# A state space scan: GpSimd's product and its sum are put behind marks that VectorE sets

## The reference, cut to what matters

```python
zxbcdt = jnp.einsum('bld,ed->ble', x_norm, in_proj_w)      # z, x_ssm, Bm, Cm, dt
dA = jnp.minimum(jnp.exp(dt * A), 0.99)
def step(h, inp):
    x_t, B_t, C_t, dA_t = inp
    h = jnp.clip(dA_t[:, :, None, None] * h + einsum('bhp,bn->bhpn', x_t, B_t), -10., 10.)
    return (h, einsum('bn,bhpn->bhp', C_t, h))
_, y = lax.scan(step, 0, (x, B, C, dA))                    # 2048 steps, 4 heads of 64, state of 64
y = y + x_multi * Dparam[None, None, :, None]              # the product D times x and its sum
y = layernorm(y * silu(z)) ; y = layernorm(clip(einsum(y, out_proj_w)))
```

## Time and profile before

| | |
|---|---|
| median of 3 runs | 1819.15 us (1818.82 to 1821.85) |
| the profiled execution: own time | 1810.79 us |
| its span | 1808.7 us |
| mean granted TensorE clock | 0.975 of full speed |
| TensorE busy | 1701.5 us (94%) |
| VectorE busy | 1607.2 us (89%) |
| ScalarE busy | 1476.5 us (82%) |
| GpSimd busy | 653.6 us (36%) |
| sums L1862, 16 of them | 25.4 us |

### The profile page before, as it was taken

One profiled execution on the slowest core, in us unless ns is written; L12 is line 12 of the kernel. 1 busy time (PEld: TensorE's weight loads), 2 busy tenths in 40 slices (PEclk: granted clock), 3 DMA queues, 4 the chain that ended last, 5 costly groups with the idle time before them and its releaser, 6 DMA issues.

```text
span 1808.7 us, 40081 instructions
## 1 busy us (share of the span) xinstructions
PE 1701.5 (94%) x15396; PEld 658.2 (36%) x15396; DVE 1607.2 (89%) x2294; ACT 1476.5 (82%) x2806; POOL 653.6 (36%) x932
## 2 busy tenths in 40 slices
PE   6899999999999999999999999999999799899784
PEld 4432222222222222278622222222222345466553
DVE  7899999999999999945499999999997587699778
ACT  5679999999999999943399999999999567767455
POOL 1433310222444444100045565556501133133437
PEclk9999999999999999999999999999999999899798
DMA  4523222111221122278512211221102343422121
GB/s 127 175 71 85 87 65 69 57 58 35 71 61 56 57 67 66 73 209 228 143 51 64 55 45 52 59 63 47 41 10 58 90 134 97 138 65 63 42 63 47
DMA packets 152765, 142.15 MB, mean 79 GB/s; under 512 B 40394, under 2 KB 131533, under 8 KB 152418
## 3 DMA queue, kind: packets, MB, share of 16 engines
q1 hardware_dynamic: 144226, 122.37, 23.5%
q0 software_dynamic: 8352, 17.29, 3.3%
HBM read 76.60 MB, written 60.03 MB: 76 GB/s over the span
## 4 chain that ended last, share of the span: by engine, by line
PE 77%; DVE 10%; ACT 9%; issue 2%; POOL 1%; DMA 0%; POOLq 0%; DVEq 0%; ACTq 0%
PE PS L2027 30%; PE PS L2126 18%; PE PS L2011 11%; ACT probs L1347 6%; PE PS L2076 4%; PE PS L2061 2%; PE PS L2170 1%; PE PS L2176 1%; PE PS L2249 1%; DVE mxp L907 1%; DVE hst L1119 1%; PE PS L2053 1%; DVE VP L1094 1%; DVE MXV L1125 1%; PE PS L2331 1%
## 5 line engine op out<-in xcount | busy, mean ns | idle before, releaser
L907 DVE TENSOR_REDUCE mxp<-PS 128x1 f32<-128x1024 f32 x1024 | 1170.1, 1212 | 16.3 <-PE PS L2011 10.4
L1347 ACT ACTIVATE probs<-PS 128x512 f32<-128x512 f32 x2048 | 1096.3, 597 | 61.2 <-PE PS L2126 14.7
L2027 PE MATMUL PS<-probs,VH 128*32 128x256 f32 x8192 | 642.5, 391 | 1.8 <-ACT probs L1347 1.0
L2126 PE MATMUL PS<-stacks 51*128 51x512 bf16 x2048 | 438.5, 387 | 20.2 <-ACT probs L1347 16.4
L2011 PE MATMUL PS<-stacks 48*128 48x512 bf16 x2048 | 416.2, 380 | 2.2 <-DVE mxp L907 1.2
L2027 PEld LDWEIGHTS PS<-probs,VH 128*32 128x32 f32 x8192 | 173.1, 108 | 412.1 <-issue 229.7
L2126 PEld LDWEIGHTS PS<-stacks 51*128 51x128 bf16 x2048 | 115.0, 93 | 460.0 <-ACT probs L1347 421.5
L1713 POOL DMA_INDIRECT S<-oe_d,ROWI x128 | 130.0, 1015 | 130.0 <-PE PS L2027 124.1
L1683 POOL DMA_INDIRECT xe_d<-S,ROWI x128 | 125.4, 980 | 135.7 <-PE PS L2027 113.9
L1661 POOL CAST spl<-nmx 128x8 bf16<-128x8 f32 x64 | 12.7, 199 | 304.8 <-DVE nmx L863 226.6
L2011 PEld LDWEIGHTS PS<-stacks 48*128 48x128 bf16 x2048 | 106.0, 95 | 10.5 <-DVE mxp L907 5.8
(11 more groups left out here) (363 smaller groups left out, 1852.1 us busy)
## 6 DMA issues: line engine op xcount, KB each, us to landing
stacks<-qkl_d SPq DMA_DIRECT2D x128, 96.0 KB
xe_d<-zt SPq DMA_DIRECT2D x16, 640.0 KB
XNT<-xe_d SPq DMA_DIRECT2D x32, 320.0 KB, 3.8
oe_d<-XNT SPq DMA_DIRECT2D x32, 320.0 KB, 3.2
stacks<-qkl_d SPq DMA_DIRECT2D x128, 64.0 KB
o_d<-SG SPq DMA_DIRECT2D x256, 32.0 KB
ews<-in_ew_dram SPq DMA_DIRECT2D x33, 192.0 KB, 2.4
stacks<-qkl_d SPq DMA_DIRECT2D x128, 32.0 KB
```

What stands on the lines that cost most here:

```text
L907: v.tensor_reduce(mxp[:, n // 2, n % 2:n % 2 + 1], MXB[n % 2].rearrange("p a c -> p (a c)"), X_AX, ALU.max).then_inc(mx_done, 1)
L1347: act.activation(probs[:, at:at + 512], PS[:, bank_of(u, e), :], ACT.Exp, scale=float(1.0 / np.sqrt(np.float32(DK)))).then_inc(exp_done, 1)
L2027: mm = pe.matmul(OB[32 * jg:32 * jg + 32, c:c + 256], VH[w][:, kt, :], probs[:, at:at + 256], start=(kt < 2 and half == 0), stop=(kt >= TC ...
L2126: pe.matmul(PS[:, bank_of(u, e), :], KS[w][o:o + KROWS + 3, kt * P:(kt + 1) * P], QS[w][o:o + KROWS + 3, q0:q0 + 512], start=True, stop=Tr ...
```

## The change

GpSimd's two operations per chunk are put elsewhere in time, and their order on its queue is changed. VectorE marks the end of the second L1106 (operand B made) on `bd_set`, and the end of L1119 (state scaled) on `hst_set`. Both are semaphores of the attention stage used again, which stand at 64 by then (`HALVES`). The product for chunk c waits for `bd_set` of chunk c. The sum for chunk c waits for `hst_set` of chunk c besides `y_out`. The product for chunk c+1 is issued ahead of the sum for c. VectorE's wait behind L1119 is now on `hst_set` and not on its own chain. The arithmetic is the same.

```diff
+        bd_set, hst_set, HALVES = nmx_ready, spl_ready, 2 * UNITS
...
                 for b in range(B):
                     bb = BS[c % 4][:, b, :].unsqueeze(1).broadcast_to([P, NH1, DS])
-                    v.tensor_tensor(BD[w][:, b, :, :], DE[:, b * NH1:(b + 1) * NH1, P - 1:P].broadcast_to([P, NH1, DS]), bb, ALU.mult)
+                    ins = v.tensor_tensor(BD[w][:, b, :, :], DE[:, b * NH1:(b + 1) * NH1, P - 1:P].broadcast_to([P, NH1, DS]), bb, ALU.mult)
+                ins.then_inc(bd_set, 1)
...
             def chunk_state(c):
-                link(v.tensor_tensor(hst2[:, :, :], HS[:, :, :], E2[c % 2][:, :, P - 1:P].broadcast_to([P, NH1, HP]), ALU.mult))
+                v.tensor_tensor(hst2[:, :, :], HS[:, :, :], E2[c % 2][:, :, P - 1:P].broadcast_to([P, NH1, HP]), ALU.mult).then_inc(hst_set, 1)
+                v.wait_ge(hst_set, HALVES + c + 1)
                 v.wait_ge(y_out, c + 1)
...
+            by_batch = lambda t: t.rearrange("p (b n) -> p b n", b=B)
+
+            def scaled_x(c):
+                pool.wait_ge(tile_ld[c % 4], TILE_BASE + 96 * (c // 4 + 1))
+                after(pool, xd_done, XD_BASE + c - 1 if c >= 2 else 0)
+                pool.wait_ge(bd_set, HALVES + c + 1)
+                pool.tensor_tensor(by_batch(XD[c % 2]), by_batch(XS[c % 4]), sc_aff[:, 0, :].unsqueeze(1).broadcast_to([P, B, DI]), ALU.mult).then_inc(xd_made, 1)
+
+            scaled_x(0)
             for c in range(TCH):
-                xd, w = XD[c % 2], c % 4
-                pool.wait_ge(tile_ld[w], TILE_BASE + 96 * (c // 4 + 1))
-                after(pool, xd_done, XD_BASE + c - 1 if c >= 2 else 0)
-                pool.tensor_tensor(xd.rearrange("p (b n) -> p b n", b=B), XS[w].rearrange("p (b n) -> p b n", b=B),
-                                   sc_aff[:, 0, :].unsqueeze(1).broadcast_to([P, B, DI]), ALU.mult).then_inc(xd_made, 1)
+                if c + 1 < TCH:
+                    scaled_x(c + 1)
                 pool.wait_ge(xd_made, XM_BASE + c + 1)
                 pool.wait_ge(y_out, c + 1)
+                pool.wait_ge(hst_set, HALVES + c + 1)
                 yc = YS.rearrange("p (b c) n -> p b c n", b=B)[:, :, c, :]
-                pool.tensor_tensor(yc, yc, xd.rearrange("p (b n) -> p b n", b=B), ALU.add).then_inc(xd_done, 1)
+                pool.tensor_tensor(yc, yc, by_batch(XD[c % 2]), ALU.add).then_inc(xd_done, 1)
```

## The result

The changed kernel took 1807.99 us, median of 5 runs (1803.81 to 1809.53), against 1819.15 before (5 runs, 1816.38 to 1823.96): a ratio of 0.9929, 95% interval 0.9908 to 0.995. Two repetitions gave 0.9945 (0.9927 to 0.9962) and 0.9941 (0.9918 to 0.9964). So the change is 10 to 13 us faster by the three ratios, and the 6.4 us forecast were too few; 1807.99 lies just under the range (1808.5 to 1816.5). The kernel before spreads over 13 us from run to run (1812.2 to 1825.59 in one set of 20 later runs), the changed one over 7 (1803.81 to 1810.99 in 9), which the three runs shown before did not reveal.

What follows compares the result with a forecast made beforehand. TensorE, at 8.09 us a chunk, was taken to bound the scan, just above VectorE. Removed waits of 4.89 us plus 1.53 us in the last chunk gave 6.4 us: 1819.15 to 1812.7 us, range 1808.5 to 1816.5.

Steps and rivals of the forecast that it cites:

- The bound: Scan of block 1: TensorE's own 8.09 us a chunk sets the period, just above VectorE's 8.0 us.
- Rival (a): VectorE bounds the scan and all its lost time returns, 16.1 to about 19 us: 1800 to 1803 us; chance 0.05.
- L1119's hold and the slack: Scan chunks: L1119 falls from 1.48 to 0.41 us; VectorE idles 1.16 us, the state has 1.25 us to spare.
- 4.89 + 1.53: Gain in us: six TensorE waits inside the scan vanish (4.89), and the last chunk's wait shrinks (1.53).
- Rival (c): The hold only moves, from L1119 to L1121 or L1125: about 1817 us; chance 0.10 with other small-gain ways.
- The indirect DMAs: L1094, held beside GpSimd's two indirect DMAs, ends 2.09 us late, under 2.41, so the 1.42 us wait vanishes.
- The clock: Last chunk: TensorE's clock still falls in the 2.03 us gap; waits of 1.42 us and less do not lower it.
- the term 0: Clock gain taken as 0 for the last chunk, with up to 3.1 us kept for the range.
- Rival (d): Slower: the clock falls inside the scan, 5.0 us per chunk, 1822.7 us with two such chunks; chance 0.04.
- Ahead of the scan: Chunk 0, before TensorE reaches L2329: L1116 may be held by 0.3 us, counted as nothing.
- The range: Whole kernel: 1808.5 us, clock holding in the last chunk with 1 us of spread, up to 1816.5 us.

Runs made afterwards that it cites:

- product-only kernel: Changed kernel with only the product waiting, for bd_set and ahead of the sum, while the sum starts with y_out as before: 1808.73 us, ratio 0.9946.
- the sum alone: Changed kernel with only the sum waiting for hst_set and the product back behind the previous chunk's sum, without bd_set: 1804.85 us, ratio 0.9928.
- the filled kernel before: Kernel before the change with three unused 128 x 512 matmuls on TensorE in front of the last chunk's: 1812.6 us, ratio 0.9976.
- the one with the delay in series: Changed kernel with one unused VectorE instruction of 1.2 us per chunk between L1121 and the new state: median 1818.86 us.
- the one with a single gap: Changed kernel with 2 us of unused VectorE work before the new state of chunk 2 only: median 1811.74 us, ratio 0.9965.

## Why the prediction was right or wrong

**The bound, right.** TensorE's quiet chunk is 8.09 us in every profile in which VectorE is the faster one, and 19 us of added VectorE work left it there. Rival (a), 16 us and more, did not come.

**L1119's hold and the slack, right.** The scaled state (now L1121) takes 0.42 us, VectorE idles 1.03 us (1.16 forecast), the state matmul starts 2.82 us after the last L1113 (2.81 forecast). All six waits within the scan went, and the last fell from 3.56 to 2.04 (2.03 forecast). Together 8.45 - 2.04 = 6.41 us against 4.89 + 1.53. Rival (c) fell: L1124 and L1128 run beside the sum at 0.42 and 0.68 us each, as L1121 and L1125 did.

**The indirect DMAs: right result, wrong reason.** I had read that the DMAs hold L1094. In the product-only kernel L1095 began 0.47 us after the start of the second DMA (0.46 before), with no product behind it, and took 1.23 us. With the sum alone, where a product does stand behind the DMAs, VectorE was held again, this time in operand B (2.59 us for two instructions of 0.75 together):

```profile
1629.71 1.03 POOL L1875 DMA_INDIRECT ews<-in_ew_dram,rows  x1 [0.30 <-issue]
1630.18 1.23 DVE L1095 TENSOR_TENSOR VP<-cst,ldc 128x1024 f32<-128x1024 f32 x1
```

```profile
1628.50 2.59 DVE L1107 TENSOR_TENSOR YM<-VP,probs 128x256 f32<-128x256 f32 x2
1629.51 1.29 POOL L1860 TENSOR_TENSOR VH<-SG,sc_aff 128x512 f32<-128x512 f32 x1
```

So the hold came from the product queued directly behind them. What the Trainium skill infers in SBUF — State Buffer, Who interferes with whom, that a tensor_tensor leaves descriptor generation alone, agrees with the first of these rows (1.03 us beside L1095). It doesn't agree with four other profiles, in which the second DMA took 2.08 or 2.09 us beside L1103 (last section).

**The clock, wrong.** The step that failed is the sentence that the gaps of 1.42 us and less did not bring the clock down, and with it the term 0. It rested on one execution. Of three profiles of the kernel before, two have the clock down inside the scan, for 6.8 and 10.2 us; so have the filled kernel before (6.8), the one with the delay in series (10.2) and the one with a single gap (10.2). Of eight profiles of kernels without a wait over 1 us there, six have none and two 3.4 us, in the router's chunk both times. Three profiles of each kernel give 129.95 and 120.75 us, 9.2 less: 6.15 us of waits (8.19 to 2.04), 0.4 us that stand behind them in the first profile too, with the clock up (some 0.07 at each of six), and 2.6 us of clock, which I had at nothing. The last chunk gave 0.4 us more (7.42 to 6.99). Rival (d) had this mechanism with the sign reversed: it stood in the kernel before, and the change took it away.

**Ahead of the scan, put at nothing without a reason.** For chunk 0 I had weighed only a hold of L1116. But the first product held L1070: 0.51, 0.40 and 1.03 us in the three profiles of the kernel before, 0.16 in the three of the changed one. TensorE's wait before the second sums fell from 1.55 us on average to 1.14, and from chunk 0's turning matmul to the first state matmul it took 7.9 us before and 6.6 after. That is 1.3 us, most of it clock: it was down in this stretch in all three of the one and in one of the three of the other. The sum is 9.2 + 0.4 + 1.3 = 10.9 us, against 10 to 13 by the ratios, whose intervals reach from 6.5 to 17 us.

**The range.** It ended 0.5 us above the measured median. Its lower end took the clock's gain for the last chunk only, and 1 us of spread, less than the runs have.

What stays open is how often the clock falls in the unprofiled runs, and so what it is worth on average; the profiles are too few for more than some 3 us. That a wait brings it down is shown by no single profile: five of six with a wait over 1 us against two of eight without is what speaks for it, and all five fell in the router's chunk, whose small matmuls may have a part in it (two kernels fell there without such a wait). Only the fall behind the indirect DMAs, after 1.47 us of waiting, came in another chunk. A wait put back in a chunk without the router's rows was not tried. The 1.3 us ahead of the scan rest on three profiles of each kernel as well.

## What to carry to other kernels

Two engines that are within a few per cent of each other hide what the second one loses, until a disturbance uses up the slack: price such a hold by the waits it lets through, not by its length. And price a wait of TensorE by its length plus what its clock may lose behind it, from more than one execution. Put GpSimd's two-input operations where VectorE waits or reads PSUM, the one first whose collision lies on the way to the state (here the sum, which made the whole gain), and order both queues so that neither holds the other back.

## What the runs showed of the hardware

A single wait of 1.42 us was followed by 10.2 us at 1.2 GHz and cost 6.2 us; in the first profile of the kernel before waits of 1.42, 1.16 and 0.88 us cost 0.07 us beyond themselves. Whether the clock falls differs between executions of the same program.

A small copy of 8 elements with one SBUF input was held 1.0 us by GpSimd's product, where instructions with one input in PSUM and one in SBUF were never held (0.42 us each for L1121 and L1124). The Trainium skill says that a copy can run in a 2-port mode and then contends with GpSimd (SBUF — State Buffer, Who interferes with whom). The copy's 0.16 against 1.13 us agrees; which mode it ran in no row shows. A subtraction of 16 elements on one partition (L1070) was held up to 0.87 us by a product of 1.27.

Of GpSimd's indirect DMAs the second started 0.03 to 0.04 us after L1103 in eight profiles. In four of them it took 2.08 or 2.09 us and ended 0.9 us after L1103, in the other four it took 1.03 us and L1103 1.28 or 1.29 instead of 1.22. So the two seem to exclude each other at the DMA's start; what decides which one waits stays open.
